# A selective scan's seed moved from VectorE to GpSimd and ScalarE, with a matmul of its own

## The chip, the cores and the metric

The kernel runs on one core of one Trainium2 chip. The time is the device time of one execution in microseconds (us). The core's engines are named PE (TensorE, the matrix unit), DVE (VectorE), ACT (ScalarE), POOL (GpSimd) and SP (SyncE). Each has its own queue of instructions and they meet by semaphores.

## The reference, cut to what matters

The program is a Mamba block followed by a gated feed-forward block, over 4 batches of 2048 tokens, 256 wide. The change touches only the scan in the middle:

```python
def step(h, inputs):
    d_t, B_t, C_t, u_t = inputs
    dA = jnp.exp(d_t[:, :, None] * A)                       # decay
    h = h * dA + (d_t * u_t)[:, :, None] * B_t[:, None, :]  # state
    y_t = jnp.einsum('bdn,bn->bd', h, C_t)                  # output
    return (h, y_t)
```

There are 512 channels (d) with 64 states (n) each, so 32,768 independent recurrences over 2048 tokens, in each of 4 batches.

## The kernel before

Four stages run one after the other: a norm stage, a projection stage, the scan stage (`scan_stage`) and an output stage. The scan stage works in **chunks** of T = 32 tokens, 256 chunks in all, four in the body of each hardware loop. A chunk has 8 **tiles**, numbered k = 0 to 7. A tile holds 32 pairs of channels (two channels times 64 states fill the 128 partitions) by 32 tokens, so 128 x 1024 elements. `n` counts tiles over the whole stage, `f` counts chunks, and `s` is the chunk's parity.

For tile n the work goes round the engines like this:

- PE multiplies step sizes by A into `a_bank` (L806, 4 matmuls, two halves of the bank).
- ACT takes exp of it into `decay` (L849, two activations, one for each half).
- POOL multiplies the decay of the first token by the state that the previous chunk left and writes `carry` (L918). It then overwrites the decay of the first token with zero (L921), so that the scan restarts at each of the 32 pairs. Only a tile of POOL's (k = 3) also lays the window of C for the output matmuls (L908).
- PE multiplies the inputs into `u_bank` (L816, 8 matmuls), one of two halves in turn. It waits until the scan of tile n - 2 has finished with that half.
- DVE adds `carry` to the first token of each pair in `u_bank` (L879, 128 x 32) and then runs one scan over the 1024 elements (L883).
- PE contracts the finished state of the previous chunk with C into `y_bank` (L789): 8 steps, spread over the tiles by the table `CONTRACT`, with no step at k = 0, two at k = 2 and one at each other k. A step is written as 4 matmuls and stands in the trace as 8.

ACT also copies the output of a chunk out of `y_bank` (`take_y`, L835, at k = 1) and issues four DMAs that store it (`store_y`, L841, at k = 3). Each engine's order is simply the order of the code. The order on PE inside a tile is L806, L816, L789. The `decay` ring has 4 places, `a_bank` is written again once the exp of the same half has read it, and the state `H` has one buffer for each parity.

Of the kernel before, what the change touches and what calls it, by code (L numbers as in the profile page):

```python
# [22 lines left out]
ALU = mybir.AluOpType  # L23
ACT = mybir.ActivationFunctionType
# [34 lines left out]
CPS = 4  # L59
Y_PAD = TW  # L60
NG = DI // P
Y_TILE = 1
Y_STORE = 3
CONTRACT = {1: (0,), 2: (1, 2), 3: (3,), 4: (4,), 5: (5,), 6: (6,), 7: (7,)}

# [630 lines left out]
def scan_stage(nc, d):  # L696

    with ExitStack() as ctx:  # L698
        def sb(name, shape, dt=F32):
            return ctx.enter_context(nc.sbuf_tensor(name, shape, dt))  # L700
# [4 lines left out]
        H = [sb(f"s_h{s}", [P, PAIRS, T]) for s in range(2)]  # L705
        decay = sb("s_decay", [P, RING, PT, T])
        carry = sb("s_carry", [P, CPS, PT])
        none = sb("s_none", [P, PT])
        x1 = sb("s_x1", [P, 2, ROWS, HALVES, SLOTS, 2 * T], BF16)
        x2 = sb("s_x2", [P, 2, 8, 4, PAIRS], BF16)  # L710
# [4 lines left out]
        yout = sb("s_y", [P, 2, PAIRS])  # L715
        a_bank = ctx.enter_context(nc.psum_tensor("s_abank", [P, 2, GP, ROWS, T], F32))
        u_bank = ctx.enter_context(nc.psum_tensor("s_ubank", [P, 2, PT, T], F32))
        y_bank = ctx.enter_context(nc.psum_tensor("s_ybank", [P, 2, 512], F32))

        rows_loaded = [sem("rows_loaded0"), sem("rows_loaded1")]  # L720
        u_loaded = [sem("u_rows_loaded0"), sem("u_rows_loaded1")]
# [4 lines left out]
        exp_done = sem("decay_ready")  # L726
        u_ready = sem("dbu_ready")
        carried = sem("carried")
        added = sem("carry_added")
        scan_done = sem("scan_done")  # L730
        window_ready = sem("window_ready")
        y_ready = sem("y_ready")
# [39 lines left out]
        @block.tensor  # L772
        def _(pe):
            pe.sem_inc(u_ready, 16)
            pe.sem_inc(a_ready, 64)
            pe.wait_ge(y_read, 1)
            pe.sem_inc(y_ready, 1)
            pe.wait_ge(a_loaded, 16)

            def contract(f, s, parts):  # L780

                if 0 in parts:
                    pe.wait_ge(scan_done, f * TILES + 4)
                    pe.wait_ge(window_ready, f * 2 + 6)
                    pe.wait_ge(y_read, f + 1)
                for tt in parts:
                    for ct in range(4):
                        t = ct * WSTEPS + tt
                        last = nc.tensor.matmul(y_bank[32 * ct:32 * ct + WIN, s, 0:PAIRS],  # L789
                                                window[:, s, t * WIN:(t + 1) * WIN], H[s][:, :, t],  # L790
                                                start=(tt == 0), stop=(tt == WSTEPS - 1))
                if WSTEPS - 1 in parts:
                    last.then_inc(y_ready, 1)

            def chunk(it, f, c):
                s, g = c % 2, c // 2
                for k in range(TILES):
                    n = f * TILES + k
                    half, j0 = k // 4, 4 * (k % 4)
                    if k == 0 and c % 2 == 0:  # L800
                        pe.wait_ge(rows_loaded[g], it * 176 + 176)
                    for b in range(2):
                        pe.wait_ge(exp_done, n * 2 + b + 1)
                        for jj in range(GP):
                            j = j0 + GP * b + jj
                            last = nc.tensor.matmul(a_bank[:, b, jj], a_w[:, half, j, :],  # L806
                                                    x1[:, g, :, half, j, s * T:(s + 1) * T], start=True, stop=True)
                        last.then_inc(a_ready, 1)
                    if k == 0:
                        pe.wait_ge(u_loaded[s], it * 256 + (c // 2) * 128 + 128)  # L810
                    pe.wait_ge(scan_done, n + 3)
                    for b in range(2):
                        q = PT * k + 16 * b
                        for e in range(4):
                            dst = u_bank[:, k % 2, 16 * b:16 * b + 16, 8 * e:8 * e + 8]
                            last = nc.tensor.matmul(dst.rearrange("p q t -> p t q"), w2[:, g, 4 * s + e, :],  # L816
                                                    x2[:, s, :, e, q:q + 16], start=True, stop=True)
                    last.then_inc(u_ready, 1)
                    if k in CONTRACT:
                        contract(f, 1 - s, CONTRACT[k])  # L820

            over_chunks(pe, chunk)
            contract(NF, 1, tuple(range(WSTEPS)))

        @block.scalar
        def _(act):
            act.sem_inc(exp_done, 2)
            for s in range(2):
                act.sem_inc(y_stored[s], 64)

            def take_y(f, s):

                act.wait_ge(y_ready, f + 1)
                act.wait_ge(y_stored[s], (f - s) * 32 + 64)
                nc.scalar.activation(yout[:, s, :], y_bank[:, s, 0:PAIRS], ACT.Identity).then_inc(y_read, 1)  # L835

            def store_y(f, s):
                act.wait_ge(y_read, f + 2)
                for ct in range(4):
                    dst = d["y"][bass.ds(f * T + (Y_PAD - 2 * T + ct * WSTEPS), WSTEPS), :].rearrange("t (h q) -> (t h) q", h=2)  # L840
                    act.dma_start(dst, yout[32 * ct:32 * ct + WIN, s, :]).then_inc(y_stored[s], 16)  # L841

            def chunk(it, f, c):
                for k in range(TILES):
                    n = f * TILES + k
                    act.wait_ge(scan_done, n + 1)
                    for b in range(2):
                        act.wait_ge(a_ready, n * 2 + b + 65)
                        nc.scalar.activation(decay[:, k % RING, 16 * b:16 * b + 16, :],  # L849
                                             a_bank[:, b].rearrange("p j r t -> p (j r) t"),  # L850
                                             ACT.Exp).then_inc(exp_done, 1)
                    if k == Y_TILE:
                        take_y(f, c % 2)
                    if k == Y_STORE:
                        store_y(f, c % 2)

            over_chunks(act, chunk)
            for f in (NF, NF + 1):
                take_y(f, f % 2)
                store_y(f, f % 2)  # L860
            for s in range(2):
                act.wait_ge(y_stored[s], 64 * (NF // 2 + 2))

        @block.vector
        def _(dve):
            nc.vector.memset(y_bank[:, :, :], 0.0).then_inc(y_read, 1)
            nc.vector.memset(w2[:, :, :, :], 0.0).then_inc(cleared, 1)
            nc.vector.memset(x2[:, :, :, :, :], 0.0).then_inc(cleared, 1)
            nc.vector.memset(window[:, :, :], 0.0).then_inc(window_ready, 6)
            nc.vector.memset(H[1][:, :, :], 0.0).then_inc(scan_done, 4)  # L870

            def chunk(it, f, c):
                s = c % 2
                for k in range(TILES):
                    n = f * TILES + k
                    first = u_bank[:, k % 2, :, 0]
                    dve.wait_ge(carried, n * 2 + 2)
                    dve.wait_ge(u_ready, n + 17)
                    nc.vector.tensor_tensor(first, first, carry[:, k % CPS, :], ALU.add).then_inc(added, 1)  # L879
                    if k == 0:  # L880
                        dve.wait_ge(y_ready, f + 1)
                    dve.wait_ge(added, n + 1)
                    nc.vector.tensor_tensor_scan(  # L883
                        H[s][:, PT * k:PT * k + PT, :].rearrange("p q t -> p (q t)"),
                        decay[:, k % RING].rearrange("p q t -> p (q t)"),
                        u_bank[:, k % 2].rearrange("p q t -> p (q t)"), 0.0,
                        ALU.mult, ALU.add).then_inc(scan_done, 1)

            over_chunks(dve, chunk)

        @block.gpsimd
        def _(pool):
# [5 lines left out]
            def lay_window(it, f, c, n):  # L898
                s, g = c % 2, c // 2
                pool.wait_ge(rows_loaded[g], it * 176 + 176)  # L900
                pool.wait_ge(y_ready, f + 1)
                pool.wait_ge(carried, n * 2 + 2)
                for h in range(2):
                    w = window[NS * h:NS * h + NS, s, :]
                    dst = bass.AP(w.tensor, w.offset + h, [list(w.ap[0]), [WSTEPS * WIN, T // WSTEPS], [WIN + 2, WSTEPS]])
# [6 lines left out]
            def chunk(it, f, c, fresh=False):  # L912
                s = c % 2
                for k in range(TILES):
                    n = f * TILES + k
                    before = none[:, :] if fresh else H[1 - s][:, PT * k:PT * k + PT, T - 1]
                    pool.wait_ge(exp_done, n * 2 + 4)
                    nc.gpsimd.tensor_tensor(carry[:, k % CPS, :], decay[:, k % RING, :, 0], before,  # L918
                                            ALU.mult).then_inc(carried, 1)
                    pool.wait_ge(carried, n * 2 + 1)  # L920
                    nc.gpsimd.tensor_tensor(decay[:, k % RING, :, 0], none[:, :], none[:, :], ALU.mult).then_inc(carried, 1)  # L921
                    if k == 3:
                        lay_window(it, f, c, n)
# [343 lines left out]
```

## Time and profile before

| | |
|---|---|
| median of 3 runs | 7032.84 us (7032.73 to 7033.88) |
| profiled execution | 7032.57 us, its span 7030.4 us |
| busy over the span | PE 87%, DVE 83%, ACT 42%, POOL 24% |
| first and last scan | 1261.8 and 6346.4 us |
| granted PE clock, mean | 0.952 |

Busy shares are means over the whole span. The scan stage is the long stretch in the middle, and what bounds it is read from the order of events inside a tile.

### The profile page before, as it was taken

To read this page: it belongs to the slowest core of one execution; us is meant where nothing else is said; L and a number is where in the kernel's file an instruction comes from. 1 tells how busy PE (TensorE), PEld (TensorE's weight loads), DVE (VectorE), ACT (ScalarE), POOL (GpSimd) and SP (SyncE) were. 2 spreads that over 40 slices of the span, in tenths; PEclk is the share of its full clock that TensorE was granted. 3 is DMA by queue.
4 is the path that set the end of the run, shared out by engine and by line. 5 is a ranking of instruction groups with operands and counts; after the bars stand their busy time and mean duration, and the time that the engine had idled before them with its cause. 6 is when DMAs were issued, how large, how long until landed. Compare 5 with 4: busy or idle time off the path is not lost. (4 is left out here: it accounts for less than half of the span.)

```text
span 7030.4 us, 150993 instructions
## 1 busy us (share of the span) xinstructions
PE 6124.9 (87%) x46048; PEld 3347.2 (48%) x46048; DVE 5847.0 (83%) x5536; ACT 2985.0 (42%) x5218; POOL 1657.6 (24%) x4800
## 2 busy tenths in 40 slices
PE   2666553899999999999999999999999999997999
PEld 1222221455555555555555555555555555554666
DVE  7455544899999999999999999999999999994443
ACT  1544443344444444444444444444444444441111
POOL 4222223222222222222222222222222222220000
PEclk9777776999999999999999999999999999998999
DMA  4454556111111111111111111111111111113231
GB/s 136 153 168 167 178 193 202 36 32 35 33 36 33 33 35 32 35 33 36 33 33 35 32 36 33 34 34 33 35 32 36 33 34 34 32 31 119 98 116 60
DMA packets 1133035, 451.75 MB, mean 64 GB/s; under 512 B 762544, under 2 KB 1088816, under 8 KB 1132608
## 3 DMA queue, kind: packets, MB, share of 16 engines
q1 hardware_dynamic: 1088304, 421.73, 22.7%
q10 hardware_dynamic: 44688, 29.50, 1.3%
q8 instruction: 21, 0.34, 0.0%
q14 instruction: 22, 0.18, 0.0%
HBM read 229.72 MB, written 221.71 MB: 64 GB/s over the span
## 5 line engine op out<-in xcount | busy, mean ns | idle before, releaser
L883 DVE TENSOR_TENSOR_SCAN s_h<-s_decay,s_ubank 128x1024 f32<-128x1024 f32 x2048 | 4682.1, 2286 | 70.4
L849 ACT ACTIVATE s_decay<-s_abank 128x512 f32<-128x512 f32 x4096 | 2224.2, 595 | 2728.9 <-PE s_abank L806 2728.0
L816 PE MATMUL s_ubank<-s_x,s_w 128*128 128x128 bf16 x16384 | 2129.7, 309 | 195.2 <-DVE s_h L883 192.1
L789 PE MATMUL s_ybank<-s_h,s_window 128*16 128x256 f32 x16448 | 2088.8, 599 | 2.7 <-DVE s_h L883 2.7
L816 PEld LDWEIGHTS s_ubank<-s_x,s_w 128*128 128x128 bf16 x16384 | 1697.3, 129 | 340.0 <-DVE s_h L883 264.1
L918 POOL TENSOR_TENSOR s_carry<-s_decay,s_h 128x32 f32<-128x32 f32 x2016 | 588.9, 292 | 3594.4 <-ACT s_decay L849 3594.4
L806 PEld LDWEIGHTS s_abank<-s_x,s_a 128*128 128x128 bf16 x8192 | 647.1, 100 | 1638.9 <-ACT s_decay L849 1076.3
L806 PE MATMUL s_abank<-s_x,s_a 128*128 128x256 bf16 x8192 | 1270.6, 277 | 55.5 <-DMA s_w<-scratch_b_rows 55.5
L789 PEld LDWEIGHTS s_ybank<-s_h,s_window 128*16 128x16 f32 x16448 | 305.1, 97 | 534.3 <-issue 530.7
L921 POOL TENSOR_TENSOR s_decay<-s_none 128x32 f32<-128x32 f32 x2048 | 506.0, 247 | 160.3
L879 DVE TENSOR_TENSOR s_ubank<-s_ubank,s_carry 128x32 f32<-128x32 f32 x2048 | 368.9, 180 | 125.2 <-POOL s_decay L921 98.6
L499 PE MATMUL p_turn<-p_ident,p_uparts 128*128 128x128 bf16 x816 | 97.8, 309 | 407.3 <-ACT p_u_turn L579 312.6
L609 DVE TENSOR_SCALAR p_acc<-p_xi,p_conv_w 128x512 f32<-128x512 f32 x64 | 31.3, 489 | 334.7 <-ACT p_xi L532 334.7
L499 PEld LDWEIGHTS p_turn<-p_ident,p_uparts 128*128 128x128 bf16 x816 | 79.7, 141 | 444.6 <-ACT p_u_turn L579 322.0
L1093 PE MATMUL o_gu<-o_xparts,o_wgu 128*128 128x512 bf16 x1152 | 257.6, 379 | 22.2 <-DVE o_hid L1196 22.2
L469 PE MATMUL p_in<-xnT,p_w_in 128*128 (+1 forms) x512 | 228.5, 603 | 15.8 <-DMA p_b_dt<-in_b_dt 12.5
L1137 ACT ACTIVATE o_sg<-o_gu 128x512 f32<-128x512 f32 x96 | 57.3, 597 | 410.2 <-PE o_gu L1093 408.0
L579 ACT ACTIVATE p_u_turn<-p_turn 128x1024 bf16<-128x1024 bf16 x102 | 98.9, 1022 | 277.2 <-DMA scratch_b_rows<-p_b_turn 270.1
L1093 PEld LDWEIGHTS o_gu<-o_xparts,o_wgu 128*128 128x128 bf16 x1152 | 110.9, 98 | 159.1 <-DVE o_hid L1196 33.0
L1103 PE MATMUL o_ob<-o_wd,o_hid 128*128 128x256 f32 x768 | 170.0, 381 | 10.6 <-DVE o_hid L1196 10.6
L478 PE MATMUL p_bk<-p_u,p_w_x 128*128 128x512 f32 (+1 forms) x384 | 170.7, 597 | 0.0
L469 PEld LDWEIGHTS p_in<-xnT,p_w_in 128*128 128x128 f32 x512 | 97.8, 195 | 135.5 <-issue 111.8
(116 smaller groups left out, 2852.9 us busy)
## 6 DMA issues: line engine op xcount, KB each, us to landing
scratch_u_rows<-p_u_turn SPq DMA_DIRECT2D x136, 512.0 KB, 6.9
scratch_delta_rows<-p_dparts SPq DMA_DIRECT2D x128, 512.0 KB, 5.7
s_x<-scratch_delta_rows SPq DMA_DIRECT2D x1024, 64.0 KB, 3.6
s_x<-scratch_u_rows SPq DMA_DIRECT2D x2048, 32.0 KB, 1.7
scratch_y<-s_y ACTq DMA_DIRECT2D x1032, 16.0 KB, 1.5
scratch_sz<-p_sz SPq DMA_DIRECT2D x16, 1024.0 KB, 8.7
scratch_u<-p_u SPq DMA_DIRECT2D x16, 1024.0 KB, 10.0
s_w<-scratch_b_rows SPq DMA_DIRECT2D x256, 64.0 KB, 2.4
```

The costliest lines, as they stand in the source:

```text
L469: last = nc.tensor.matmul(in_bank[:, m % 2, :], w_in[:, k, m * P:(m + 1) * P], xnT[:, k, bass.ds(i * TW, TW)], start=(k == 0), stop=(k == ...
L478: last = nc.tensor.matmul(bk_bank[0:n, bank, :], w_x[:, m, lo:lo + n], u[:, c % 2, m, :], start=(m == 0), stop=(m == MI - 1))
L499: last = nc.tensor.transpose(turn_bank[:, g % 2, n * P:(n + 1) * P], src, ident[:, :])
L789: last = nc.tensor.matmul(y_bank[32 * ct:32 * ct + WIN, s, 0:PAIRS], window[:, s, t * WIN:(t + 1) * WIN], H[s][:, :, t], start=(tt == 0), ...
L806: last = nc.tensor.matmul(a_bank[:, b, jj], a_w[:, half, j, :], x1[:, g, :, half, j, s * T:(s + 1) * T], start=True, stop=True)
L816: last = nc.tensor.matmul(dst.rearrange("p q t -> p t q"), w2[:, g, 4 * s + e, :], x2[:, s, :, e, q:q + 16], start=True, stop=True)
L849: nc.scalar.activation(decay[:, k % RING, 16 * b:16 * b + 16, :], a_bank[:, b].rearrange("p j r t -> p (j r) t"), ACT.Exp).then_inc(exp_do ...
L879: nc.vector.tensor_tensor(first, first, carry[:, k % CPS, :], ALU.add).then_inc(added, 1)
L883: nc.vector.tensor_tensor_scan(H[s][:, PT * k:PT * k + PT, :].rearrange("p q t -> p (q t)"), decay[:, k % RING].rearrange("p q t -> p (q t)"),
L918: nc.gpsimd.tensor_tensor(carry[:, k % CPS, :], decay[:, k % RING, :, 0], before, ALU.mult).then_inc(carried, 1)
L921: nc.gpsimd.tensor_tensor(decay[:, k % RING, :, 0], none[:, :], none[:, :], ALU.mult).then_inc(carried, 1)
L1093: last = nc.tensor.matmul(gu[:, m % 2, r, :], wgu[:, r, kk, m * P:(m + 1) * P], xparts[:, part, kk, :], start=(n == 0), stop=(n == 3 * KD ...
```

## The change

The first token's input is computed once more for all 256 pairs of a chunk, by one matmul into a bank of its own (`first_bank`). ACT copies it to SBUF (`first`). POOL adds `carry` to it and writes `seed`. ACT then writes `seed` over the first token of each pair in `u_bank`, and DVE's add is gone. `y_bank` shrinks from two banks to one to make room, so a contraction waits until the output before it has been copied out, and `take_y` moves to k = 0.

```diff
-                    pe.wait_ge(y_read, f + 1)
+                    pe.wait_ge(y_read, f + 2)
...
                     if k == 0:
                         pe.wait_ge(u_loaded[s], it * 256 + (c // 2) * 128 + 128)
+                        pe.wait_ge(first_read, f + 1)
+                        nc.tensor.matmul(first_bank[:, 0:PAIRS], w2[:, g, 4 * s, :], x2[:, s, 0, 0, :],
+                                         start=True, stop=True).then_inc(first_ready, 1)
...
-                    if k == Y_TILE:
+                    if k == 0:
+                        act.wait_ge(first_ready, f + 1)
+                        nc.scalar.activation(first[:, c % 2, :], first_bank[:, 0:PAIRS],
+                                             ACT.Identity).then_inc(first_read, 1)
                         take_y(f, c % 2)
+                    act.wait_ge(u_ready, n + 17)
+                    act.wait_ge(carried, n * 3 + 3)
+                    nc.scalar.activation(u_bank[:, k % 2, :, 0], seed[:, k % CPS, :], ACT.Identity).then_inc(seeded, 1)
                     if k == Y_STORE:
                         store_y(f, c % 2)
...
-                    first = u_bank[:, k % 2, :, 0]
-                    dve.wait_ge(carried, n * 2 + 2)
-                    dve.wait_ge(u_ready, n + 17)
-                    nc.vector.tensor_tensor(first, first, carry[:, k % CPS, :], ALU.add).then_inc(added, 1)
                     if k == 0:
                         dve.wait_ge(y_ready, f + 1)
-                    dve.wait_ge(added, n + 1)
+                    dve.wait_ge(seeded, n + 1)
...
-                    pool.wait_ge(carried, n * 2 + 1)
+                    if k == 0:
+                        pool.wait_ge(first_read, f + 2)
+                    pool.wait_ge(carried, n * 3 + 1)
+                    nc.gpsimd.tensor_tensor(seed[:, k % CPS, :], carry[:, k % CPS, :],
+                                            first[:, s, PT * k:PT * k + PT], ALU.add).then_inc(carried, 1)
                     nc.gpsimd.tensor_tensor(decay[:, k % RING, :, 0], none[:, :], none[:, :], ALU.mult).then_inc(carried, 1)
```

ACT's queue from the exps of tile k = 3 to the exps of k = 4, before:

```order
L849 ACTIVATE s_decay<-s_abank 128x512 [waits a_ready]
L848 REGISTER_ALU
L849 ACTIVATE s_decay<-s_abank 128x512 [waits a_ready]
L838 REGISTER_ALU
L841 ISA [waits y_read]
L841 DMA scratch_y<-s_y 16x256
L841 ISA
```

Three more DMA rows follow there, then L846 and L848 for the next tile. The same place now (line numbers are the changed kernel's, `carried` is POOL's semaphore, `dbu_ready` is that of `u_bank`):

```order
L857 ACTIVATE s_decay<-s_abank 128x512 [waits a_ready]
L856 REGISTER_ALU
L857 ACTIVATE s_decay<-s_abank 128x512 [waits a_ready]
L865 REGISTER_ALU
L866 ISA [waits dbu_ready]
L867 ACTIVATE s_ubank<-s_seed 128x32 [waits carried]
L846 REGISTER_ALU
L849 ISA [waits y_read]
L849 DMA scratch_y<-s_y 16x256
L849 ISA
```

A small activation that waits for POOL now stands between a tile's exps and everything behind them: at k = 3 the four DMA issues, at every k the exps of the next tile.

POOL's queue for one tile, before:

```order
L917 ISA
L918 TENSOR_TENSOR s_carry<-s_decay,s_h 128x32 [waits decay_ready]
L920 REGISTER_ALU
L921 TENSOR_TENSOR s_decay<-s_none 128x32 [waits carried]
```

And now:

```order
L927 ISA
L928 TENSOR_TENSOR s_carry<-s_decay,s_h 128x32 [waits decay_ready]
L932 ISA
L933 TENSOR_TENSOR s_seed<-s_carry,s_first 128x32 [waits carried]
L935 TENSOR_TENSOR s_decay<-s_none 128x32
```

The add stands between the two operations that were there, and ACT waits for the last of the three.

## Rows read from the trace of the kernel before

**Rows 1.** The page's costliest groups: busy us, mean ns, then idle before.

```profile
L883 DVE TENSOR_TENSOR_SCAN s_h<-s_decay,s_ubank 128x1024 f32<-128x1024 f32 x2048 | 4682.1, 2286 | 70.4
...
L921 POOL TENSOR_TENSOR s_decay<-s_none 128x32 f32<-128x32 f32 x2048 | 506.0, 247 | 160.3
L879 DVE TENSOR_TENSOR s_ubank<-s_ubank,s_carry 128x32 f32<-128x32 f32 x2048 | 368.9, 180 | 125.2 <-POOL s_decay L921 98.6
```

**Rows 2.** One line's view: the scans, duration and first and last start.

```profile
L883 DVE TENSOR_TENSOR_SCAN s_h<-s_decay,s_ubank x2048: 2286/2286/2289, 1261.8 to 6346.4; 128x1024 f32<-128x1024 f32 x187
```

**Rows 3.** Windows: stretch, then PE, PEld, DVE, ACT, POOL busy, granted clock, DMA.

```profile
700.00:1350.00 650.00, 343.40 (x1667) 169.85 (x1668) 342.05 (x273) 260.08 (x345) 186.43 (x123) 0.72 0.50 163
1350.00:6500.00 5150.00, 4920.56 (x40802) 2667.98 (x40800) 4883.74 (x4128) 2353.66 (x4369) 1222.14 (x4542) 1.00 0.17 37
```

**Rows 4.** Timeline of an ordinary tile: start, length (us), engine, line.

```profile
3503.42 0.61 PE L806 MATMUL s_abank<-s_x,s_a 128*128 128x256 bf16 x4
...
3503.70 2.29 DVE L883 TENSOR_TENSOR_SCAN s_h<-s_decay,s_ubank 128x1024 f32<-128x1024 f32 x1
...
3503.85 1.09 ACT L849 ACTIVATE s_decay<-s_abank 128x512 f32<-128x512 f32 x2 [1.30 <-PE s_abank L806]
3503.87 1.04 PE L816 MATMUL s_ubank<-s_x,s_w 128*128 128x128 bf16 x8
...
3505.02 0.29 POOL L918 TENSOR_TENSOR s_carry<-s_decay,s_h 128x32 f32<-128x32 f32 x1 [1.77 <-ACT s_decay L849]
...
3505.39 0.25 POOL L921 TENSOR_TENSOR s_decay<-s_none 128x32 f32<-128x32 f32 x1
...
3505.81 0.61 PE L806 MATMUL s_abank<-s_x,s_a 128*128 128x256 bf16 x4
...
3506.11 2.29 DVE L883 TENSOR_TENSOR_SCAN s_h<-s_decay,s_ubank 128x1024 f32<-128x1024 f32 x1
```

**Rows 5.** Timeline of the same chunk boundary, on to tile k = 4.

```profile
3508.45 1.05 PE L816 MATMUL s_ubank<-s_x,s_w 128*128 128x128 bf16 x8 [0.68 <-DVE s_h L883]
...
3508.52 2.29 DVE L883 TENSOR_TENSOR_SCAN s_h<-s_decay,s_ubank 128x1024 f32<-128x1024 f32 x1
...
3510.86 1.05 PE L816 MATMUL s_ubank<-s_x,s_w 128*128 128x128 bf16 x8
...
3511.84 1.90 PE L789 MATMUL s_ybank<-s_h,s_window 128*16 128x256 f32 x16
...
3513.67 0.61 PE L806 MATMUL s_abank<-s_x,s_a 128*128 128x256 bf16 x4
...
3514.10 0.60 ACT L849 ACTIVATE s_decay<-s_abank 128x512 f32<-128x512 f32 x1 [2.19 <-PE s_abank L806]
3514.55 0.32 ACTq L841 DMA_DIRECT2D scratch_y<-s_y  x1
...
3515.05 1.29 ACTq L841 DMA_DIRECT2D scratch_y<-s_y  x3
...
3516.01 0.20 DVE L879 TENSOR_TENSOR s_ubank<-s_ubank,s_carry 128x32 f32<-128x32 f32 x1 [0.38 <-POOL s_decay L921]
...
3516.24 2.29 DVE L883 TENSOR_TENSOR_SCAN s_h<-s_decay,s_ubank 128x1024 f32<-128x1024 f32 x1
...
3516.54 0.60 ACT L849 ACTIVATE s_decay<-s_abank 128x512 f32<-128x512 f32 x1 [1.35 <-PE s_abank L806]
```

**Rows 6.** ACT's sequencer operations of L848, from 3511 to 3514.3 us.

```profile
L848 ACTq FUSED_REGOPS  x1: 37/37/37, 3511.1 to 3511.1; - x1
...
L848 ACTq ALU_OP  x1: 35/35/35, 3514.1 to 3514.1; - x1
```

**Rows 7.** Timeline of ACT at the start of a loop body.

```profile
4041.87 1.28 ACT L849 ACT_TABLE_LOAD   x1
4043.16 1.08 ACT L849 ACTIVATE s_decay<-s_abank 128x512 f32<-128x512 f32 x2
```

**Rows 8.** Groups of instructions on ACT: the copy out of `y_bank`.

```profile
L835 ACT ACTIVATE s_y<-s_ybank 128x256 f32<-128x256 f32 x258 | 101.3, 393 | 10.4 <-PE s_ybank L789 10.4
```

More of the change, by code:

```diff
@@ L61 @@
 NG = DI // P
-Y_TILE = 1
 Y_STORE = 3
@@ L707, in scan_stage @@
         carry = sb("s_carry", [P, CPS, PT])
+        first = sb("s_first", [P, 2, PAIRS])
+        seed = sb("s_seed", [P, CPS, PT])
         none = sb("s_none", [P, PT])
@@ L717, in scan_stage @@
         u_bank = ctx.enter_context(nc.psum_tensor("s_ubank", [P, 2, PT, T], F32))
-        y_bank = ctx.enter_context(nc.psum_tensor("s_ybank", [P, 2, 512], F32))
+        y_bank = ctx.enter_context(nc.psum_tensor("s_ybank", [P, 512], F32))
+        first_bank = ctx.enter_context(nc.psum_tensor("s_firstbank", [P, 512], F32))
         rows_loaded = [sem("rows_loaded0"), sem("rows_loaded1")]
@@ L728, in scan_stage @@
         carried = sem("carried")
-        added = sem("carry_added")
+        first_ready = sem("first_ready")
+        first_read = sem("first_read")
+        seeded = sem("seeded")
         scan_done = sem("scan_done")
@@ L788, in contract @@
                         t = ct * WSTEPS + tt
-                        last = nc.tensor.matmul(y_bank[32 * ct:32 * ct + WIN, s, 0:PAIRS],
+                        last = nc.tensor.matmul(y_bank[32 * ct:32 * ct + WIN, 0:PAIRS],
                                                 window[:, s, t * WIN:(t + 1) * WIN], H[s][:, :, t],
@@ L827, in _ @@
             act.sem_inc(exp_done, 2)
+            act.sem_inc(first_read, 1)
             for s in range(2):
@@ L834, in take_y @@
                 act.wait_ge(y_stored[s], (f - s) * 32 + 64)
-                nc.scalar.activation(yout[:, s, :], y_bank[:, s, 0:PAIRS], ACT.Identity).then_inc(y_read, 1)
+                nc.scalar.activation(yout[:, s, :], y_bank[:, 0:PAIRS], ACT.Identity).then_inc(y_read, 1)
             def store_y(f, s):
@@ L865, in _ @@
         def _(dve):
-            nc.vector.memset(y_bank[:, :, :], 0.0).then_inc(y_read, 1)
+            nc.vector.memset(y_bank[:, :], 0.0).then_inc(y_read, 1)
             nc.vector.memset(w2[:, :, :, :], 0.0).then_inc(cleared, 1)
@@ L901, in lay_window @@
                 pool.wait_ge(y_ready, f + 1)
-                pool.wait_ge(carried, n * 2 + 2)
+                pool.wait_ge(carried, n * 3 + 3)
                 for h in range(2):
```

## The prediction, made before the changed kernel ran

> **What bounds the kernel now.** I read the page first, then windows, then the timeline of one chunk. The scan stage runs from 1261.8 to 6346.4 us [rows 2]. That is 2047 tile steps, 2.484 us each, so 19.87 us for a chunk of 8. DVE needs 2.286 us for a scan and 0.18 us for the add in front of it [rows 1], together 2.466, so DVE is all but full. It looks as if 0.18 us a tile could be had. Two things in the timeline say how little room there is behind DVE.
>
> First, PE. From one L806 to the next it takes 3505.81 - 3503.42 = 2.39 us in an ordinary tile, with no wait in it, while DVE's scans stand 3506.11 - 3503.70 = 2.41 us apart [rows 4]. PE catches its breath only at the start of a chunk, where it waits 0.68 us for a scan, and at k = 2, with two contraction steps, it falls behind: the scan there starts 3516.24 - 3508.52 = 7.72 us after the scan of k = 0, where three tiles at DVE's pace would be 7.24 [rows 5].
>
> Second, ACT and POOL. They are mostly idle, but each tile passes through them in series. The exps start at 3503.85, POOL's carry at 3505.02 and its zeroing at 3505.39, ending at 3505.64 [rows 4]. So POOL is done 1.79 us after the exps began. Today that costs ACT nothing, since it goes on to the next exps as soon as PE delivers.
>
> **The change part by part.**
>
> The add leaves DVE. Bound: the pace falls from 2.41 us to the scan's 2.29, 0.13 us a tile. It is worth something only if nothing else ends later.
>
> The extra matmul has 256 columns like those of L806, whose four take 0.61 us [rows 4]: some 0.15 us of PE a chunk. It falls at k = 0, where PE waits 0.68 us [rows 5], so nothing. If that cover is gone it costs 0.15 x 256 = 38 us. The copy of `first_bank` is like L835, 0.39 us [rows 8]. It stands on ACT behind the exps of k = 0 while POOL makes `carry`, and ends about 1.09 + 0.39 = 1.5 us after the exps began. POOL would begin its new add at 1.17 + 0.37 = 1.54. So nothing, and at most 0.1 us if it is late. `take_y` follows and ends before 1.9, before POOL is through. The single `y_bank` makes PE wait for that `take_y`; the contraction needs it only at k = 1, over 2 us later: nothing.
>
> The new cycle, which is what I expect to decide. ACT's write of `seed` waits for three POOL operations of the same tile, and the next exps are queued behind it. So ACT can no longer start tile n + 1 until POOL is done with tile n. With the exps' start as zero:
> - carry starts at 1.17 [rows 4]. POOL's operations start 0.37 apart [rows 4]. One more puts the zeroing's end at 1.79 + 0.37 = 2.16. If the zeroing, which has no wait of its own now, follows at once, one length of 0.25 replaces the step: 2.04. I take 2.10.
> - From POOL to ACT I take 0.08, the step from ACT to POOL (3503.85 + 1.09 to 3505.02) [rows 4], with 0.04 and 0.12 as ends. The seed write starts at 2.18.
> - Its length: a 512-column activation takes 0.60 [rows 5] and a 256-column one 0.39 [rows 8], so 32 columns come to about 0.21.
> - The next exp follows the seed's start by about 0.20, the step from the last DMA issue's end (3515.05 + 1.29) to the exp at 3516.54 [rows 5]; ends 0.17 and 0.25.
>
> The cycle is 2.38 us (2.25 to 2.50 with all ends). PE's 2.39 and this one are alike, so ordinary tiles hardly gain over 2.41.
>
> At k = 3. ACT's four DMA issues now stand behind the seed write. What such a wait does to the issuing side: ACT's sequencer made its last operation of that line at 3511.1, then nothing until 3514.1 [rows 6], the moment when the exp that had waited for PE started (3514.10) [rows 5]. It does not pass an activation that is still waiting. From the first issue to the next exp takes 3516.54 - 3514.55 = 1.99 us [rows 5]. Before, this ran while PE worked. Now it begins when the seed write is released at 2.18, plus 0.20 to 0.45 until the first issue (0.45 is the step from the exp at 3514.10 to the issue, with a second exp in it [rows 5]); I take 0.23. So the exps of k = 4 come 2.18 + 0.23 + 1.99 = 4.40 us after those of k = 3, instead of 2.44. Queued behind them are POOL's work and the scan of k = 4, which waits for it.
>
> The Trainium skill says otherwise (Perfetto Trace Analysis, "DVE / Act Engine Instruction"): an instruction is pushed into a wait queue, and the sequencer is then ready to fetch the next one. By that rule the DMA issues would run during the seed's wait and the 1.96 us would not arise. The trace does not agree [rows 6]; it is the second rival.
>
> At k = 0 to 3. The exps of k = 3 need PE's L806, which comes after u and two contraction steps of k = 2, and u waits for the scan of k = 0. The scan of k = 0 starts at 2.18 + 0.21 + 0.03 (the step from DVE's add to its scan, 3516.01 + 0.20 to 3516.24) = 2.42 and ends at 4.71. Then 0.05 to PE (3506.11 + 2.29 [rows 4] to 3508.45), 2.81 (3510.86 to 3513.67) and 0.43 (to 3514.10) [rows 5]: 8.00 us from exps to exps. Three cycles would be 7.14, so this is the longer one. It is also longer than the 7.72 of today, since the way from POOL to the scan now goes over ACT.
>
> The table load. ACT loads its tables once in a loop body of 4 chunks, 1.28 us [rows 7]. Today it fits in the gap while ACT waits for PE. Now it stands between a seed write and the next exps, on the cycle: 1.28 plus the seed's own 0.21 less the 0.20 already counted, and some loop operations, 1.4 us, or 0.35 a chunk.
>
> Sum for a chunk: 8.00 (k = 0 to 3) + 4.40 (3 to 4) + 4 x 2.38 (4 to 8) + 0.35 = 22.27 us, against 19.87. That is +2.40 x 256 = +614 us. The profiled execution took 7032.57 us, 0.3 us from the median of the runs, so both give 7647. **I predict 7645 us**, 8.7% slower.
>
> Bounds: with all short ends, 7.90 + 4.27 + 4 x 2.39 (PE's pace then holds) + 0.3 = 22.0, or 7580. If PE keeps a lead there and the cycle is 2.25, 21.5, or 7450. With all long ends, 8.10 + 4.72 + 10.0 + 0.4 = 23.2, or 7890.
>
> **The rivals.**
> 1. *Faster: the scans set the pace.* If the cycle over ACT and POOL is hidden, as its idle shares allow (ACT is busy 2354 of 5150 us [rows 3]), DVE runs at 2.29 and PE becomes the bound. PE has 19.87 - 0.68 + 0.15 = 19.34 us of work in a chunk, so -0.53 x 256: 6897 us. It decides once seed writes are released before the scan ahead of them ends, also at k = 4, and that needs a cycle under 2.3 and issues that are over in time. Against it: the steps of the cycle are in series by semaphores, and I count 2.38 without the issues. Chance 0.04.
> 2. *The sequencer passes the waiting seed write.* The step from 3 to 4 then takes about a cycle, 2.44: 22.27 - 1.96 = 20.31, +0.44 x 256: 7145 us. Chance 0.08.
> 3. *Same.* Gains and losses cancel: this needs rival 2 and no table load on the path. Chance 0.03.
> 4. *Slower still.* The short operations are dearer than their neighbours (cycle of 2.6: 4 x 0.22 + 0.4 = +1.3 a chunk), 7980 us. A PE clock below full goes here too: it was 0.72 where PE was busy 53% of the time and 1.00 in the scan stage at 96% [rows 3]; I expect 86%, between the two. At 0.9 the PE part of k = 0 to 3 costs 0.3 us a chunk, 7720 us. Chance of a time above 7820: 0.1.
>
> My forecast, everything from 7500 to 7820, has the rest, 0.75.
>
> **How the numbers follow.** A measurement of this kernel can tell about 0.2%, 14 us, from no change. Slower by more: 0.75 + 0.1 + 0.08 = 0.93. Within: 0.03. Faster: 0.04. The range leaves out both faster cases, rival 2 and the upper half of rival 4: 7500 to 7850.
>
> **What the profile of the changed kernel would show.** Right: the exps of k = 4 about 4.4 us after those of k = 3, with the DMA issues starting only after the seed write; the seed write waiting for POOL's zeroing in nearly every tile; scans waiting for ACT's seed write, in sum some 0.2 us in ordinary tiles and 2 us at k = 4; exps no longer waiting for PE except at k = 3; the table load directly between a seed write and an exp. DVE's busy time falls by 369 us and its idle time grows by some 980. Wrong: DMA issues that begin before the seed write starts (rival 2), a seed write of 0.4 us or a POOL add much over 0.3 us (rival 4), or scans back to back (rival 1).

## The result, and the profile after

The changed kernel takes 7701.89 us (median of 4, 7698.55 to 7703.28) against 7032.78 us for the kernel before. The ratio is 1.095, 95% interval 1.093 to 1.097: 669 us slower. I had predicted 7645 us, with 7500 to 7850 as the range.

From the page of the changed kernel, the groups that answer to [rows 1] (busy us, mean ns, then idle before them and what ended it):

```profile
L893 DVE TENSOR_TENSOR_SCAN s_h<-s_decay,s_ubank 128x1024 f32<-128x1024 f32 x2048 | 4604.7, 2280 | 1173.3 <-ACT s_ubank L867 1131.5
...
L867 ACT ACTIVATE s_ubank<-s_seed 128x32 f32<-128x32 f32 x2048 | 412.0, 201 | 1778.0 <-POOL s_decay L935 1776.8
```

DVE lost its 369 us of adds and stands idle for 1173 us instead of 196, nearly all of it for ACT's seed write. That write takes 0.20 us and waits for POOL in all but one tile, 0.87 us on the mean (1776.8 us over 2047 waits). The first scan starts at 1262.8 and the last at 7013.6 us, so a chunk takes 5750.8 / 2047 x 8 = 22.47 us (before: 19.87).

Where in the chunk it goes is in the timeline. ACT and POOL around k = 3 and 4 (start, length in us):

```profile
3518.55 1.08 ACT L857 ACTIVATE s_decay<-s_abank 128x512 f32<-128x512 f32 x2 [1.25 <-PE s_abank L810]
3519.71 0.29 POOL L928 TENSOR_TENSOR s_carry<-s_decay,s_h 128x32 f32<-128x32 f32 x1 [2.64 <-ACT s_decay L857]
3520.08 0.25 POOL L933 TENSOR_TENSOR s_seed<-s_carry,s_first 128x32 f32<-128x32 f32 x1
3520.29 0.25 POOL L935 TENSOR_TENSOR s_decay<-s_none 128x32 f32<-128x32 f32 x1
3520.57 0.20 ACT L867 ACTIVATE s_ubank<-s_seed 128x32 f32<-128x32 f32 x1 [0.94 <-POOL s_decay L935]
...
3520.79 1.81 ACTq L849 DMA_DIRECT2D scratch_y<-s_y  x4
...
3522.80 1.08 ACT L857 ACTIVATE s_decay<-s_abank 128x512 f32<-128x512 f32 x2 [2.02 <-issue]
...
3524.82 0.20 ACT L867 ACTIVATE s_ubank<-s_seed 128x32 f32<-128x32 f32 x1 [0.93 <-POOL s_decay L935]
3524.98 1.08 ACT L857 ACTIVATE s_decay<-s_abank 128x512 f32<-128x512 f32 x2
```

Two readings. The whole step is visible at 3520.57: the seed write starts when POOL is done, the four issues start 0.22 us later (in each of the stage's chunks the first of them starts 0.22 us or more after the seed write does, never before it), and the next exps start when they are over, 4.25 us after the exps of k = 3 (3518.55 to 3522.80). And the plain cycle is 3522.80 to 3524.98, 2.18 us: shorter than the 2.38 I had counted.

ACT's exps over the rest of a chunk, k = 6, 7, 0, 1, 2, 3 and 4:

```profile
3527.16 1.09 ACT L857 ACTIVATE s_decay<-s_abank 128x512 f32<-128x512 f32 x2
...
3529.77 1.08 ACT L857 ACTIVATE s_decay<-s_abank 128x512 f32<-128x512 f32 x2 [0.38 <-PE s_abank L810]
...
3532.16 1.09 ACT L857 ACTIVATE s_decay<-s_abank 128x512 f32<-128x512 f32 x2 [0.16 <-PE s_abank L810]
...
3534.34 1.08 ACT L857 ACTIVATE s_decay<-s_abank 128x512 f32<-128x512 f32 x2
...
3536.75 1.08 ACT L857 ACTIVATE s_decay<-s_abank 128x512 f32<-128x512 f32 x2 [0.19 <-PE s_abank L810]
...
3540.00 1.08 ACT L857 ACTIVATE s_decay<-s_abank 128x512 f32<-128x512 f32 x2 [1.02 <-PE s_abank L810]
...
3544.24 1.08 ACT L857 ACTIVATE s_decay<-s_abank 128x512 f32<-128x512 f32 x2 [2.02 <-issue]
```

From k = 4 (3522.80) to k = 4 of the next chunk is 21.44 us. The mean is 22.47, so once in four chunks 4 x 22.47 - 4 x 21.44 = 4.1 us are added. They are at the end of ACT's loop body, k = 7 to k = 0:

```profile
3504.48 1.08 ACT L857 ACTIVATE s_decay<-s_abank 128x512 f32<-128x512 f32 x2 [0.39 <-PE s_abank L810]
3506.50 0.20 ACT L867 ACTIVATE s_ubank<-s_seed 128x32 f32<-128x32 f32 x1 [0.94 <-POOL s_decay L935]
3509.42 1.28 ACT L857 ACT_TABLE_LOAD   x1 [2.72 <-DVE s_h L893]
3510.72 1.08 ACT L857 ACTIVATE s_decay<-s_abank 128x512 f32<-128x512 f32 x2
```

The load that I had counted follows a pause of 2.72 us that I had not. The timeline names a scan as its releaser. ACT's sequencer tells more; its operations of the loop's line from 3506 to 3510 us (name, count, duration in ns, first and last start):

```profile
L744 ACTq COMPARE_BRANCH  x1: 45/45/45, 3506.6 to 3506.6; - x1
...
L744 ACTq FUSED_REGOPS  x1: 59/59/59, 3509.3 to 3509.3; - x1
```

The branch back runs at 3506.6, and the very next operation, which waits for nothing, starts at 3509.3. The page's row of the instruction queue, which had 22 packets before, and the same row for the pause alone (3506.5 to 3509.4 us):

```profile
q14 instruction: 352, 2.88, 0.1%
...
q14 instruction: 2, 0.02, 1.4%
```

### The profile page after: what moved, and what is told of

Read it like the earlier page. It is cut to its first block and busy times, and to the rows that moved or that the text cites. A ratio compares the mean times of both kernels' runs of the same rounds, so it can differ in the third digit from the quotient of the medians.

```text
span 7696.7 us, 154290 instructions
## 1 busy us (share of the span) xinstructions
PE 6323.3 (82%) x46272; PEld 3400.2 (44%) x46304; DVE 5535.7 (72%) x3488; ACT 3436.7 (45%) x7522; POOL 2088.0 (27%) x6848
## 5 line engine op out<-in xcount | busy, mean ns | idle before, releaser
L893 DVE TENSOR_TENSOR_SCAN s_h<-s_decay,s_ubank 128x1024 f32<-128x1024 f32 x2048 | 4604.7, 2280 | 1173.3 <-ACT s_ubank L867 1131.5
L823 PE MATMUL s_ubank<-s_x,s_w 128*128 128x128 bf16 x16384 | 2180.8, 315 | 299.6 <-DVE s_h L893 299.6
L823 PEld LDWEIGHTS s_ubank<-s_x,s_w 128*128 128x128 bf16 x16384 | 1732.6, 131 | 486.8 <-DVE s_h L893 430.0
L810 PE MATMUL s_abank<-s_x,s_a 128*128 128x256 bf16 x8192 | 1335.0, 281 | 415.3 <-ACT s_decay L857 332.1
L867 ACT ACTIVATE s_ubank<-s_seed 128x32 f32<-128x32 f32 x2048 | 412.0, 201 | 1778.0 <-POOL s_decay L935 1776.8
L933 POOL TENSOR_TENSOR s_seed<-s_carry,s_first 128x32 f32<-128x32 f32 x2048 | 516.2, 252 | 163.5 <-ACT s_first L862 3.1
```

Of the source, the lines that this page charges most:

```text
L867: nc.scalar.activation(u_bank[:, k % 2, :, 0], seed[:, k % CPS, :], ACT.Identity).then_inc(seeded, 1)
L893: nc.vector.tensor_tensor_scan(H[s][:, PT * k:PT * k + PT, :].rearrange("p q t -> p (q t)"), decay[:, k % RING].rearrange("p q t -> p (q t)"),
L933: nc.gpsimd.tensor_tensor(seed[:, k % CPS, :], carry[:, k % CPS, :], first[:, s, PT * k:PT * k + PT], ALU.add).then_inc(carried, 1)
```

## The experiments

Kernels of a group ran on one chip beside the kernel before. Its median there is 7028.74 us for e1, e2, e3 and e7, 7029.13 for e4, e5, e6 and e8, and 7029.48 for e9, e10 and e11. The changed kernel itself did not run again in these groups; where a run is compared with its 7701.89 us, some 4 us of the difference (7032.78 against 7028.74) may come from that. "Chunk" is (last scan's start - first scan's start) / 2047 x 8. All intervals are 95%.

| run | us | ratio to before | chunk, us |
|---|---|---|---|
| stores ahead of the seed write (e1) | 7359.16 | 1.047 (1.045 to 1.049) | 21.15 |
| stores issued by SP (e2) | 7096.48 | 1.010 (1.008 to 1.011) | 20.11 |
| ACT's loop body of 2 chunks (e3) | 7615.22 | 1.083 (1.081 to 1.085) | 22.15 |
| before, PE order (e4) | 6974.20 | 0.992 (0.991 to 0.994) | 19.65 |
| e2 and PE order (e5) | 7046.24 | 1.003 (1.002 to 1.004) | 19.92 |
| before, no add (e6) | 6938.24 | 0.987 (0.986 to 0.989) | 19.50 |
| before, ACT's body of 8 chunks (e7) | 7089.53 | 1.009 (1.007 to 1.010) | 20.09 |
| e5, seed write waits for the add alone (e8) | 7005.31 | 0.997 (0.995 to 0.998) | 19.76 |
| e6 and PE order (e9) | 6935.60 | 0.987 (0.985 to 0.988) | 19.49 |
| e4, add doesn't wait for the zeroing (e10) | 6913.88 | 0.984 (0.982 to 0.985) | 19.41 |
| before, the extra parts alone (e11) | 7027.92 | 1.000 (0.999 to 1.001) | 19.86 |

### The DMA issues: e1 and e2

e1 swaps two blocks on ACT:

```diff
+                    if k == Y_STORE:
+                        store_y(f, c % 2)
                     act.wait_ge(u_ready, n + 17)
                     act.wait_ge(carried, n * 3 + 3)
                     nc.scalar.activation(u_bank[:, k % 2, :, 0], seed[:, k % CPS, :], ACT.Identity).then_inc(seeded, 1)
-                    if k == Y_STORE:
-                        store_y(f, c % 2)
```

> The changed kernel, with ScalarE's four DMA issues of tile k = 3 moved ahead of the seed write instead of behind it. My theory: the issues then run while GpSimd works on the same tile, so only what exceeds GpSimd's time stays on the path. The exps of k = 4 follow those of k = 3 by about 2.6 us instead of 4.24; minus 1.6 us a chunk, 256 chunks: about 7290 us (7240 to 7340). Rival, the issues were never the cause and the 4.24 us is a late exp for another reason (the seed write or GpSimd's window at k = 3): no change, 7700 us.

7359 us: 343 less, where I had expected some 410. ACT from k = 3 on in an ordinary chunk of this run:

```profile
3529.72 0.60 ACT L857 ACTIVATE s_decay<-s_abank 128x512 f32<-128x512 f32 x1 [1.02 <-PE s_abank L810]
3530.17 0.32 ACTq L849 DMA_DIRECT2D scratch_y<-s_y  x1
...
3530.66 1.29 ACTq L849 DMA_DIRECT2D scratch_y<-s_y  x3
3532.15 0.20 ACT L869 ACTIVATE s_ubank<-s_seed 128x32 f32<-128x32 f32 x1 [1.35 <-POOL s_decay L935]
3532.33 1.08 ACT L857 ACTIVATE s_decay<-s_abank 128x512 f32<-128x512 f32 x2
...
3537.11 1.08 ACT L857 ACTIVATE s_decay<-s_abank 128x512 f32<-128x512 f32 x2 [0.37 <-PE s_abank L810]
```

The seed write is now the one that waits for the issues (it names POOL, which was done at 3531.71, but the issues end at 3531.95), and the step from the exps of k = 3 to those of k = 4 is 2.61 us, as expected. Two things hold the gain back. In one chunk of the four in a loop body the issues start later and take 2.05 us instead of some 1.79, and that step is 3.0 us; over all chunks it is 2.72 on the mean, 1.52 us less than the 4.24 of the changed kernel, or 389 us. And part of this is lost again behind it: with the issues gone ACT catches up with PE, and the step from k = 5 to k = 6 is 2.59 us instead of 2.18 (the wait of 0.37 us above), of which 0.23 comes back at k = 7. The net 0.18 x 256 = 46 us explain the rest of the miss.

e2 takes them off ACT. SP issues the stores of a chunk one chunk later, behind its own loads:

```diff
+            def store_late(f, s):
+                sp.wait_ge(y_read, f + 1)
+                for ct in range(4):
+                    dst = d["y"][bass.ds(f * T + (Y_PAD - 3 * T + ct * WSTEPS), WSTEPS), :].rearrange("t (h q) -> (t h) q", h=2)
+                    sp.dma_start(dst, yout[32 * ct:32 * ct + WIN, s, :]).then_inc(y_stored[s], 16)
...
-                    if k == Y_STORE:
-                        store_y(f, c % 2)
```

> The changed kernel, with the output stores issued by SyncE's queue one chunk later, so ScalarE issues no DMA inside the loop (its loop body is shorter by those rows too). My theory: the step from the exps of k = 3 to those of k = 4 becomes a plain cycle of 2.2 to 2.4 us: minus 1.85 to 2.0 us a chunk, 7200 us (7150 to 7260). If the shorter body also takes away the 2.6 us after ScalarE's loop branch, 0.6 us a chunk more, 7040 us. Rival, the issues were not the cause: 7700 us.

7096 us, 605 less, between my two numbers. ACT at k = 3 and 4 in this run, and DVE's scans over three chunks:

```profile
3540.21 1.09 ACT L864 ACTIVATE s_decay<-s_abank 128x512 f32<-128x512 f32 x2 [1.02 <-PE s_abank L818]
3542.23 0.20 ACT L874 ACTIVATE s_ubank<-s_seed 128x32 f32<-128x32 f32 x1 [0.94 <-POOL s_decay L941]
3542.59 1.09 ACT L864 ACTIVATE s_decay<-s_abank 128x512 f32<-128x512 f32 x2 [0.16 <-PE s_abank L818]
```

```profile
3501.55 11.83 DVE L899 TENSOR_TENSOR_SCAN s_h<-s_decay,s_ubank 128x1024 f32<-128x1024 f32 x5 [0.95 <-ACT s_ubank L874]
...
3522.70 18.80 DVE L899 TENSOR_TENSOR_SCAN s_h<-s_decay,s_ubank 128x1024 f32<-128x1024 f32 x8 [1.18 <-ACT s_ubank L874]
3542.46 18.81 DVE L899 TENSOR_TENSOR_SCAN s_h<-s_decay,s_ubank 128x1024 f32<-128x1024 f32 x8 [0.95 <-ACT s_ubank L874]
```

The step is 2.38 us, and now PE ends it. A plain chunk takes 19.76 us (3522.70 to 3542.46) instead of 21.44: 1.68 x 256 = 430 us were the issues. The chunk with the loop's end takes 21.15 (3501.55 to 3522.70), so the end of the loop body costs 1.39 us in four chunks instead of 4.1: another 2.7 / 4 x 256 = 173 us, since without the issues ACT's loop body is shorter. Together 603 of the 605.

### The pause at the loop's end: e3 and e7

e3 keeps the changed kernel and gives ACT's loop two chunks a body. e7 gives the kernel before eight in place of four.

```diff
-            over_chunks(act, chunk)
+            with act.Fori(0, NF // 2) as it:      # e7: NF // 8, range(8), it * 8 + c
+                for c in range(2):
+                    chunk(it, it * 2 + c, c)
```

> The changed kernel, with ScalarE's hardware loop over 2 chunks a body instead of 4; the work and its order are the same, the table load comes twice as often. Theory A: the 2.6 us after ScalarE's loop branch come from the body's length (its instructions are fetched anew), so they vanish, the instruction queue's packets fall from 352 to about 22, and a table load costs 1.4 us each: 2.8 us per 4 chunks instead of 4.2, about 7610 us. Theory B: the table load itself waits for the scan of the tile before, as the trace's releaser says: twice as many waits, 8.4 us per 4 chunks, about 7970 us.

> The kernel before, with ScalarE's hardware loop over 8 chunks a body instead of 4; same work and order, half as many table loads. Theory A (body length): a pause of about 2.6 us appears after ScalarE's loop branch, once in 8 chunks, and the instruction queue moves some hundred packets more. ScalarE has about 1.3 us of idle time ahead of the exps there, and the table load already uses it, so 2 to 2.6 us reach the scans once in 8 chunks: plus 60 to 85 us, about 7100 us. Theory B (the pause belongs to the changed kernel's waits): no pause, 7030 us or a few us less.

Theory A holds in both: 7615 and 7090 us, where it said 7610 and 7100. With twice as many table loads e3 is 87 us faster, which the releaser's reading of the pause (the load waits for a scan) can't give. e7 shows the pause in the kernel before, which has no seed write. The loop's line on ACT's sequencer in e7, 3668 to 3672 us, and its row of the instruction queue:

```profile
L857 ACTq COMPARE_BRANCH  x1: 45/45/45, 3668.4 to 3668.4; - x1
L857 ACTq FUSED_REGOPS  x1: 59/59/59, 3671.1 to 3671.1; - x1
```

```profile
q14 instruction: 178, 1.46, 0.1%
```

That is 178 packets for 32 iterations; the changed kernel has 352 for 64, e3 and e2 have 36 and 38, the kernel before 22. From one branch of ACT's loop to the next the trace has 164 records of ACT and its sequencer in e3, 224 in the kernel before, 275 in e2, 324 in the changed kernel and in e1, and 444 in e7. The changed kernel, e1 and e7 have the pause; the others go on 0.2 us after the branch. So the pause comes with the body's length, somewhere between 275 and 324 records. By their times, two of the queue's packets, of 8 KB each, fall into nearly every pause of the changed kernel and one into nearly every pause of e7, and none stands beside a branch in e2, e3 and the kernel before. That fits a fetch of instructions; no run isolates it as the cause.

### What the add was worth: e6, e9 and e11

e6 deletes the `tensor_tensor` of the kernel before and its semaphore; the carry then no longer enters the state, so e6 and e9 leave out a part of the program. e9 is e6 with the PE order of e4. e11 adds to the kernel before the matmul into `first_bank`, its copy, the single `y_bank` and `take_y` at k = 0.

> The kernel before without VectorE's add: the carry from chunk to chunk is left out of the state, so the recurrence restarts every 32 tokens; GpSimd still computes the carry and VectorE still waits for it. It is what removing the add could bring at the very most, with no price paid on another engine. Theory: TensorE takes over at 2.39 us a tile and the stall at k = 3 stays (7.5 us for k = 0 to 3, then 5 x 2.39), 19.4 us a chunk: about 6910 us. Rival: VectorE's own pace of 2.29 us decides, 18.3 us a chunk: 6630 us.

> The kernel before without VectorE's add (the carry is left out of the state) and with the decay matmuls of the next tile ahead of the contraction steps: no stall at k = 3 and a scan that needs 2.29 us. It measures TensorE's own bound. From the rows, 19.87 minus 0.68 of waiting = 19.19 us a chunk; a few tenths are lost where TensorE waits for exps at k = 0 and 1 (0.34 us in the run with the order alone): 19.2 to 19.5, about 6880 us (6860 to 6930). Rival: VectorE's 18.3 us a chunk, 6630 us.

> The kernel before with the change's additions alone: the matmul of the first tokens, its copy to SBUF (read by nobody), one bank for the output contraction and the copy of the output at k = 0. VectorE keeps its add; GpSimd has no new operation and ScalarE writes no seed. My theory says these parts are covered: 7030 us, within 15 us (a matmul of 0.11 us a chunk uncovered would be 28 us). Rival: the single bank or the copies at k = 0 hold something up, 0.2 us a chunk or more: 7080 us and up.

e6: 6938 us (expected 6910), 91 less. That is what the removal brings with nothing paid for it, a quarter of the 369 us that DVE spends on the adds. DVE's scans from k = 0 on in that run show where the rest stays:

```profile
3505.91 6.64 DVE L880 TENSOR_TENSOR_SCAN s_h<-s_decay,s_ubank 128x1024 f32<-128x1024 f32 x3 [0.18 <-POOL s_decay L918]
3513.39 2.29 DVE L880 TENSOR_TENSOR_SCAN s_h<-s_decay,s_ubank 128x1024 f32<-128x1024 f32 x1 [0.84 <-POOL s_decay L918]
3515.92 6.92 DVE L880 TENSOR_TENSOR_SCAN s_h<-s_decay,s_ubank 128x1024 f32<-128x1024 f32 x3 [0.24 <-POOL s_decay L918]
```

Three scans close together (k = 0, 1 and 2), then 0.84 us of waiting at k = 3, where there had been 0.38 [rows 5]. A faster DVE waits longer for the same late exps. e9 takes that wait away and is no faster (6936, expected 6880): the wait moves to k = 0, where DVE idles 0.99 us a chunk, because the decay matmuls of k = 0 still stand behind a contraction step. e11 confirms the parts counted at nothing: 7027.92 against 7029.48. In the changed kernel too the seed write of k = 0, with both copies ahead of it on ACT, starts 2.02 us after its exps (3510.72 to 3512.74), as that of k = 4 does.

### The order on PE, and the best version: e4, e5, e8 and e10

e4 on PE (`decays` is the loop over the decay matmuls, taken out of the tile's head for k above 1):

```diff
                     if k in CONTRACT:
+                        if k + 1 < TILES:
+                            decays(f, k + 1, s, g)
                         contract(f, 1 - s, CONTRACT[k])
```

> The kernel before, with one change of order on TensorE: from k = 1 to k = 6 the four decay matmuls of the next tile stand ahead of the contraction steps instead of behind them. Nothing else. My theory of the 0.48 us stall at k = 3 (and of the 3.24 us at the same place in the changed kernel): the exps wait for decay matmuls queued behind two contraction steps. With them ahead, the 2.89 us between the scans of k = 2 and k = 3 becomes 2.41 and the chunk 19.30 us: about 6895 us (6880 to 6920). Rival: TensorE as a whole is the bound and the order doesn't matter; no change, 7030 us.

6974 us: faster, but 55 us of the 134 expected. The scans of k = 7, 0, 1 and 2 in e4:

```profile
3499.93 2.29 DVE L889 TENSOR_TENSOR_SCAN s_h<-s_decay,s_ubank 128x1024 f32<-128x1024 f32 x1
...
3502.45 0.20 DVE L885 TENSOR_TENSOR s_ubank<-s_ubank,s_carry 128x32 f32<-128x32 f32 x1 [0.23 <-POOL s_decay L927]
3502.68 2.29 DVE L889 TENSOR_TENSOR_SCAN s_h<-s_decay,s_ubank 128x1024 f32<-128x1024 f32 x1
...
3505.10 2.29 DVE L889 TENSOR_TENSOR_SCAN s_h<-s_decay,s_ubank 128x1024 f32<-128x1024 f32 x1
...
3507.51 2.29 DVE L889 TENSOR_TENSOR_SCAN s_h<-s_decay,s_ubank 128x1024 f32<-128x1024 f32 x1
```

The stall at k = 3 is gone, and 0.34 us of it is back at k = 0 (2.75 instead of 2.41), in front of the add. e10 lets the add start before the zeroing, which it doesn't need:

```diff
-                    dve.wait_ge(carried, n * 2 + 2)
+                    dve.wait_ge(carried, n * 2 + 1)
                     dve.wait_ge(u_ready, n + 17)
                     nc.vector.tensor_tensor(first, first, carry[:, k % CPS, :], ALU.add).then_inc(added, 1)
...
+                    dve.wait_ge(carried, n * 2 + 2)
                     dve.wait_ge(added, n + 1)
```

> The kernel before with the new order on TensorE, and VectorE's add no longer waits for GpSimd's zeroing (it needs the carry alone; the scan waits for the zeroing). In the run with the order alone the add waited 0.23 us for the zeroing at k = 0, inside a step of 2.76 us. Theory: about 0.2 us a chunk less, minus 50 us against that run: 6925 us (6915 to 6950). Rival: at k = 0 TensorE's late decay matmuls set the time and TensorE has no slack left to give: 6970 us.

6913.88 us (expected 6925), the fastest kernel of the study, 1.6% under the kernel before and 24 us under e6, which leaves the add out. Its step at k = 0 is 2.52 us:

```profile
3509.97 2.29 DVE L890 TENSOR_TENSOR_SCAN s_h<-s_decay,s_ubank 128x1024 f32<-128x1024 f32 x1
3512.17 0.19 DVE L885 TENSOR_TENSOR s_ubank<-s_ubank,s_carry 128x32 f32<-128x32 f32 x1
3512.49 2.29 DVE L890 TENSOR_TENSOR_SCAN s_h<-s_decay,s_ubank 128x1024 f32<-128x1024 f32 x1
```

e5 and e8 repair the changed kernel in the same spirit. In e8 ACT waits for `carried` at n * 3 + 2 and DVE for n * 3 + 3.

> The changed kernel with both repairs: output stores issued by SyncE, and the decay matmuls ahead of the contraction steps on TensorE. Theory: the 3.24 us at k = 3 goes, the rest is TensorE's own work, 19.3 to 19.5 us a chunk, and one table load in four chunks adds up to 0.3: 6930 us (6890 to 6980). Rival: the cycle over GpSimd and ScalarE, 2.18 to 2.20 us, is slowed by something else once TensorE is ahead, and the time stays near 7050.

> The kernel of the run above, and the seed write waits for GpSimd's add alone; VectorE waits for the zeroing itself. Theory: the cycle over ScalarE and GpSimd is 0.2 us shorter, but TensorE is the bound, so only the iteration with the table load gains: within 15 us of the run above. Rival: the cycle is the bound there; 0.2 us a tile less, 50 us or more faster.

e5 missed (7046, expected 6930). What ACT's seed write and DVE's scans wait for in e5, from 2000 to 5500 us (total us, times, longest):

```profile
ACT s_ubank L880 <- PE s_ubank L835: 1034.2, 878, 1.4
...
ACT s_ubank L880 <- POOL s_decay L947: 397.1, 527, 0.9
DVE s_h L905 <- ACT s_ubank L880: 252.6, 352, 1.5
```

DVE waits in two tiles of a chunk (352 in 3500 us; a chunk takes 19.9). The larger one is k = 0, where its scan starts at 3513.89 after 0.95 us of idle time. The contraction step of k = 7 is ahead of the decay matmuls there, and behind them stand exps, three POOL operations and the seed write in series. In five tiles of eight the seed write is held by PE's `u_bank`, which hides the cycle. e8 gained 41 us over e5, more than my 15 and less than the rival's 50. That is 0.16 us a chunk, the shortening of one cycle and not of eight: DVE's wait at k = 0 fell from 0.95 to 0.81 us, while at k = 4 to 7 PE ends the seed write's wait in both runs, 0.23 us after POOL is done in e5 (3503.04 to 3503.27). With every repair the seed's new route is still 91 us behind e10, which keeps the add.

## Why the prediction was right

The sign, the size and the main cause held. By the terms of the sum, in us a chunk:

| term | predicted | measured | from |
|---|---|---|---|
| exps k = 0 to 3 | 8.00 | 7.84 | 3532.16 to 3540.00 |
| exps k = 3 to 4 | 4.40 | 4.24 | 3540.00 to 3544.24 |
| exps k = 4 to 8 | 9.52 | 9.36 | 3522.80 to 3532.16 |
| end of ACT's loop body | 0.35 | 1.03 | 22.47 - 21.44 |
| sum | 22.27 | 22.47 | |

- **The cycle was over-sized**, 2.18 us instead of 2.38, below the low end of 2.25. POOL's zeroing, which has no wait now, starts 0.21 us after the add's start, while the add (0.25 us) still runs. I had allowed 0.25 at the least. From POOL to ACT it is 0.03 instead of 0.08 (3520.54 to 3520.57), and the next exp follows a seed write by 0.16 instead of 0.20. All three upper terms are too large for this: 0.48 x 256 = 123 us too much.
- **Why the three are not smaller still:** four bare cycles would be 8.72 us, and k = 4 to 8 took 9.36. PE ends two of the waits (0.38 and 0.16 us). That PE sits just behind, at 2.39 us a tile, was step one of the prediction.
- **The end of the loop body was under-sized** by 0.68 us a chunk, 174 us. I had the table load and not the 2.6 us pause after the branch, 0.65 us a chunk. e3, e7 and e2 show that it comes with the length of ACT's body, which the change raised from 224 records to 324.
- **The DMA issues** are the largest single term, as predicted: 1.86 us in the step (4.24 against 2.38 in e2), 1.68 us a chunk when taken away.
- **Rival 2 is out.** The issues start 0.22 us or more after the seed write does in every chunk, and e1 and e2, which take them out from behind it, are 343 and 605 us faster. The Trainium skill's rule (Perfetto Trace Analysis, "DVE / Act Engine Instruction") would let the sequencer go on once the write is in the wait queue; in this kernel it didn't: the first issue started at 3520.79, the write at 3520.57.
- **Rival 1, the scans' own pace,** is out even with nothing paid: e6 gave 91 us, and the 6897 of that rival is 41 us below it.
- **PE's clock cost a little**, the way rival 4 said and less than it feared. It was granted at 0.98 on the mean from 2000 to 5500 us, and that is not spread evenly: in 52 short stretches, 215 us in all, it stood at half of full speed, where the kernel before has no such stretch in its scan stage. Each begins 3.5 to 5.9 us after one of the 64 branches of ACT's loop, when PE has stood idle for want of exps (3.29 us before its first matmul in the one shown). This one (its row of the windows view, with the clock as third number from the end), and ACT's exps of k = 1, 2 and 3 in that chunk:

```profile
3240.00:3243.40 3.40, 2.32 (x12) 1.85 (x12) 0.72 (x1) 3.00 (x8) 0.75 (x3) 0.50 0.27 47
...
3242.61 1.08 ACT L857 ACTIVATE s_decay<-s_abank 128x512 f32<-128x512 f32 x2
...
3245.45 1.08 ACT L857 ACTIVATE s_decay<-s_abank 128x512 f32<-128x512 f32 x2 [0.61 <-PE s_abank L810]
...
3249.45 1.08 ACT L857 ACTIVATE s_decay<-s_abank 128x512 f32<-128x512 f32 x2 [1.78 <-PE s_abank L810]
```

The two steps take 6.84 us, against 5.65 behind the pause at 3506.6 (3512.90 to 3518.55), where the clock stayed at full. Over 60 loop bodies they take 6.02 on the mean in the chunk behind the pause and 5.66 in the other chunks: 0.36 us, 64 times, or 23 us. They are part of the 1.03 us in the table.
- **The signs in the profile** held for the most part: the step at k = 3, the seed write waiting for POOL, 2 us of DVE's idle time at k = 4 (1.96), and 978 us more of it in all. Two did not. Exps wait for PE not at k = 3 alone but also at k = 7, 0 and 2 (0.38, 0.16 and 0.19 us), and the table load comes 2.7 us after a seed write's end and not directly behind it.
- The parts at zero cost held (e11), and the two errors, 123 too much and 174 too little, nearly cancel. The prediction was closer than its terms: that it missed by only 57 us is in part luck.

## What to carry to other kernels

Before work moves from a full engine to idle ones, write down the cycle that it closes: here ACT waited for POOL and POOL for ACT within one tile, at 45% and 27% busy over the span. Then ask what stands behind the new wait in the same queue; four DMA issues and a table load that had been hidden, and a pause that had not been there, cost more than the operation that was saved. And measure the prize by deleting the operation (e6): it was a quarter of its busy time, and a new order of instructions that were already there (e10) brought more than the whole of it.

## What the runs showed of the hardware that I had not expected

- A hardware loop on ACT with 324 records in its body pauses 2.6 us (2.4 to 2.9) after its backward branch, and one with 444 pauses 2.4 us (2.3 to 2.7), where one with 275 goes on after 0.2. Each such iteration has about five packets more on the instruction queue ((352 - 22) / 64 and (178 - 22) / 32). The timeline put the pause down to the semaphore of a scan.
- A pause of one engine can lower the clock of another: behind it, and after 3.3 us without a matmul, PE's granted clock was at half of full speed for a while in 52 of the 64 loop bodies of the changed kernel. Eight L823 matmuls took 1.91 us there instead of 1.04.
- Two POOL operations of 0.25 us with no wait between them start 0.21 us apart; with a wait between, 0.37.
- ACT's four DMA issues took 1.79 us on the median, in the changed kernel and in e1, and 2.05 us in some chunks of e1.
